# Splitting the fp32-to-bf16 weight casts into smaller DMAs and issuing them at other places of an eight-core attention and FFN layer

## What is computed

```python
xn = layernorm(x)                                   # x: (4, 2048, 2048)
nq  = rmsnorm(xn @ w_cq);  nkv = rmsnorm(xn @ w_ckv)
q = concat(nq @ w_dq_nope, rope(nq @ w_dq_rope))    # 16 heads, 128 + 64
k = concat(nkv @ w_dk_nope, rope(xn @ w_k_rope))
v = (nkv @ w_dv) / sqrt(16 * 128)
s = softmax(causal(q @ k.T / sqrt(192))) @ v @ w_proj
h = xn @ W1.T;  q = clip(round(h / 0.1), -32768, 32767)
g = silu(gelu(q * 0.1) @ W2.T)                      # W1: 8192 x 2048, W2: 2048 x 8192
out = x + s * g
```

## Time and profile before

| | us |
|---|---|
| median of 2 runs | 8458.27 (8431.25 to 8485.28) |
| the profiled execution | 8322.42 |
| its span, slowest core (core 1) | 8320.8 |
| spans of the 8 cores | 8282.9 to 8320.8 |
| P1, from the barrier of Pm1 to the first `dknB` load of P1end | about 105 to 1276 |
| P1end, from the first matmul | about 1300 to 2024 |
| P2 of pass 0, and of pass 1 | 2087 to 3378, 5034 to 5947 |

### The profile page before, as it was taken

One profiled execution on the slowest core, in us unless ns is written; L12 is line 12 of the kernel. 1 busy time (PEld: TensorE's weight loads), 2 busy tenths in 40 slices (PEclk: granted clock), 3 DMA queues, 4 the chain that ended last, 5 costly groups with the idle time before them and its releaser, 6 DMA issues.

```text
span 8320.8 us, 74648 instructions; the slowest of 8 cores (8282.9 to 8320.8 us)
## 1 busy us (share of the span) xinstructions
PE 5338.5 (64%) x23280; PEld 2334.2 (28%) x23280; DVE 2314.3 (28%) x4548; ACT 1242.8 (15%) x2969; POOL 472.5 (6%) x571
## 2 busy tenths in 40 slices
PE   0413034554676678866666758999977767676776
PEld 0201011222232233323222323444323332332332
DVE  1101022223233334023333214344213333333321
ACT  0101001112000001011111101111012222222220
POOL 1000000000121211000000000000000000000000
PEclk9766567787888899976666779999976666666678
DMA  6598883221554443421111242222331101110114
GB/s 124 77 112 123 120 116 83 70 74 67 145 138 136 126 132 97 132 79 53 53 53 52 80 154 69 75 76 74 105 97 37 35 21 37 37 34 23 37 46 156
DMA packets 372685, 698.02 MB, mean 84 GB/s; under 512 B 161248, under 2 KB 251360, under 8 KB 364960
## 3 DMA queue, kind: packets, MB, share of 16 engines
q1 hardware_dynamic: 335104, 504.76, 20.3%
q0 software_dynamic: 37200, 188.51, 14.5%
HBM read 740.59 MB, written 178.78 MB: 110 GB/s over the span
## 4 chain that ended last, share of the span: by engine, by line
PE 52%; DMA 18%; DVE 12%; issue 6%; ACT 5%; another core or an unknown queue 5%; POOL 1%; DVEq 0%; SPq 0%; ACTq 0%; POOLq 0%
PE pb L766 5%; PE pb L772 4%; PE pb L693 4%; PE pb L699 4%; PE pb L368 4%; PE pb L370 4%; PE pb L372 4%; PE pb L1014 3%; DVE heap L977 3%; DMA heapb<-cqB 3%; PE pb L1032 2%; PE pb L959 2%; PE pb L950 2%; ACT heap L990 2%
## 5 line engine op out<-in xcount | busy, mean ns | idle before, releaser
L368 PE MATMUL pb<-heapb 128*128 128x512 bf16 (+1 forms) x1920 | 755.8, 394 | 424.9 <-DMA heapb<-dknB 283.7
L766 PE MATMUL pb<-heapb 128*128 128x512 bf16 x2048 | 796.0, 389 | 330.8 <-DMA heapb<-w2B 240.7
L379 DVE TENSOR_TENSOR heapb<-pb,heapb 128x128 bf16<-128x128 f32 (+1 forms) x1600 | 523.6, 340 | 1170.6 <-ACT heapb L377 546.5
L693 PE MATMUL pb<-heapb 128*128 128x512 bf16 x2048 | 785.2, 383 | 52.5 <-DMA heapb<-w1B 52.5
L772 PE MATMUL pb<-heapb 128*128 128x512 bf16 x2048 | 794.8, 388 | 0.8 <-POOL heapb L744 0.8
L699 PE MATMUL pb<-heapb 128*128 128x512 bf16 x2048 | 784.7, 383 | 0.0
L377 ACT ACTIVATE heapb<-pb 128x128 bf16<-128x128 f32 (+1 forms) x1600 | 488.8, 316 | 1839.7 <-PE pb L1014 1005.3
L370 PE MATMUL pb<-heapb 128*128 128x512 bf16 (+1 forms) x1920 | 753.2, 392 | 0.0
L372 PE MATMUL pb<-heapb 128*128 128x512 bf16 (+1 forms) x1920 | 750.5, 391 | 0.0
L437 PE MATMUL pb<-heap 128*128 128x128 f32 x384 | 86.7, 419 | 957.5 <-ACT heap L429 957.5
L1014 PE MATMUL pb<-heap 128*128 128x128 f32 x1280 | 457.7, 399 | 275.6 <-DVE heap L1003 275.6
(11 more groups left out here) (141 smaller groups left out, 6238.8 us busy)
## 6 DMA issues: line engine op xcount, KB each, us to landing
heapb<-w1B SPq DMA_DIRECT2D x128, 512.0 KB, 3.6
heapb<-w2B SPq DMA_DIRECT2D x512, 128.0 KB, 2.2
heapb<-prB SPq DMA_DIRECT2D x128, 512.0 KB, 4.6
heapb<-cqB SPq DMA_DIRECT2D x128, 384.0 KB, 3.8
w1B<-w1s POOLq DMA_DIRECT2D x16, 2048.0 KB, 169.6
w2B<-w2t POOLq DMA_DIRECT2D x4, 8192.0 KB, 201.6
heapb<-kkB SPq DMA_DIRECT2D x64, 512.0 KB, 3.3
heapb<-vvB SPq DMA_DIRECT2D x64, 512.0 KB, 4.7
```

What stands on the lines that cost most here:

```text
L368: p.do("tensor", lambda e: e.matmul(bank_ap, wh_ap, xh_ap, start=first, stop=False), reads=list(wbufs) + list(xbufs), writes=[pbank[n]], a ...
L379: p.do("vector", lambda e: e.tensor_tensor(lo_ap, bank_ap, hi_ap, ALU.subtract), reads=[pbank[nb], hibuf], writes=[lobuf])
L693: p.do("tensor", lambda e, kc=kc, fg=fg, bk=bk: e.matmul(banks[bk][:, 0:512], bv("AB", A_W1 + 2048 * (fg % 3) + 128 * kc, A_W1 + 2048 * (f ...
L766: p.do("tensor", lambda e, kc=kc, tt=tt: e.matmul(banks[2 + tt][:, 0:512], bv("AB", A_AP + 512 * kc + 128 * tt, A_AP + 512 * kc + 128 * (t ...
```

## The change

The 24 casts of `cast_gx` become 50, and are issued elsewhere. Sizes below are of the bf16 result. W1 stays in 16 casts of 2 MB, W2 goes from 4 of 8 MB to 16 of 2 MB, the query weights from 6, 6 and 3 MB to ten of 1.5 MB, and the projection from one of 8 MB to 8 of 1 MB. The bytes are the same.

- 12 casts of W1: one behind each token tile 4 to 15 of P1.
- The other 4 of W1: at the end of heads 0 to 3 of P1end. The 16 of W2: one at the end of heads 4 to 11, two at the end of heads 12 to 15.
- The query and projection casts: at the end of the slabs of P2 in pass 0, two each after slabs 0 to 4, three each after slabs 5 and 6, two after slab 7.

The semaphores are counted over new sets (GXA to GXF), and SyncE waits for the second half of W1 in slab 3, ahead of the load for slab 4's first block, and for the second half of W2 in slab 4. SyncE, PE, ACT and DVE keep their instructions and their order.

```diff
+            if t >= 4 and gx_p1:
+                sx, dx, semx = gx_p1.pop(0)
+                cast_gx(sx, dx, semx)
...
-        if grp == 0:
-            for fg in range(0, 64, 4):
-                cast_gx(w1t_d[fg:fg + 4], w1B[fg:fg + 4], "GXA")
-            gx_marks["w1"] = ("GXA", p.cnt.get("GXA", 0))
-        elif grp == 1:
-            for r in range(0, D_FF, 2048):
-                cast_gx(w2t_d[r:r + 2048, :], w2B[r:r + 2048, :], "GXB")
...
-        elif grp == 2:
-            cast_gx(w_cq_d[:, :], cqB[0], "GXC")
-            cast_gx(w_dqn_d[:, :, :], dqnB[0], "GXC")
-            cast_gx(w_dqr_d[:, :, :], dqrB[0], "GXC")
...
-        else:
-            cast_gx(w_pr_d[:, :], prB[0], "GXD")
...
         store(krotB[1, h], bs("AB", 0, 64, A_KROTP + 2048, A_KROTP + 4096), krotp)
+        if gx_p1:
+            sx, dx, semx = gx_p1.pop(0)
+            cast_gx(sx, dx, semx)
+        elif gx_p1end:
+            sx, dx, semx = gx_p1end.pop(0)
+            cast_gx(sx, dx, semx)
+            if h >= 12 and gx_p1end:
+                sx, dx, semx = gx_p1end.pop(0)
+                cast_gx(sx, dx, semx)
...
+                    if g == 0 and fg + 2 == 32:
+                        p.raw_wait("sync", "GXB", p.cnt.get("GXB", 0))
...
+                if g == 0 and slab == 4 and nt == 0:
+                    p.raw_wait("sync", "GXD", p.cnt.get("GXD", 0))
...
+            if g == 0:
+                for _ in range(2 if slab < 5 else 3):
+                    if gx_p2a:
+                        sx, dx, semx = gx_p2a.pop(0)
+                        cast_gx(sx, dx, semx)
+                    elif gx_p2b:
+                        sx, dx, semx = gx_p2b.pop(0)
+                        cast_gx(sx, dx, semx)
```

More of the change, by code:

```diff
@@ L357, in build_program @@
     cast_weight(w_dv_d[:, :, :], dvB[0])
-    gx_marks = {}
     def cast_gx(src_fp32, dst_bf16, sem):
@@ L363, in cast_gx @@
              reads=[], writes=[], dma=sem)
+    gx_p1 = []
+    for fg in range(0, 64, 4):
+        gx_p1.append((w1t_d[fg:fg + 4], w1B[fg:fg + 4], "GXA" if fg < 32 else "GXB"))
+    gx_p1end = []
+    for i2 in range(16):
+        r2 = 512 * i2
+        gx_p1end.append((w2t_d[r2:r2 + 512, :], w2B[r2:r2 + 512, :], "GXC" if i2 < 8 else "GXD"))
+    gx_p2a = []
+    for i2 in range(4):
+        gx_p2a.append((w_cq_d[32 * i2:32 * (i2 + 1), :], cqB[0, 32 * i2:32 * (i2 + 1), :], "GXE"))
+    for h2 in range(0, 16, 4):
+        gx_p2a.append((w_dqn_d[h2:h2 + 4], dqnB[0, h2:h2 + 4], "GXE"))
+    gx_p2a.append((w_dqr_d[0:8], dqrB[0, 0:8], "GXE"))
+    gx_p2a.append((w_dqr_d[8:16], dqrB[0, 8:16], "GXE"))
+    gx_p2b = []
+    for i2 in range(8):
+        gx_p2b.append((w_pr_d[16 * i2:16 * (i2 + 1), :], prB[0, 16 * i2:16 * (i2 + 1), :], "GXF"))
     if stop_here("PW"):
@@ L679, in build_program @@
                 if g == 0:
-                    p.raw_wait("sync", *gx_marks["w1"])
+                    p.raw_wait("sync", "GXA", p.cnt.get("GXA", 0))
                 w1_load(0)
@@ L757, in build_program @@
                 if g == 0 and slab == 0 and nt == 0:
-                    p.raw_wait("sync", *gx_marks["w2"])
+                    p.raw_wait("sync", "GXC", p.cnt.get("GXC", 0))
+                if g == 0 and slab == 4 and nt == 0:
+                    p.raw_wait("sync", "GXD", p.cnt.get("GXD", 0))
                 w2_load(0)
@@ L806, in build_program @@
         if g == 0:
-            p.raw_wait("sync", *gx_marks["cq"])
+            p.raw_wait("sync", "GXE", p.cnt.get("GXE", 0))
         cq_load(0)
@@ L881, in build_program @@
         if g == 0:
-            p.raw_wait("sync", *gx_marks["dq"])
+            p.raw_wait("sync", "GXE", p.cnt.get("GXE", 0))
         load_dq(0)
@@ L1065, in build_program @@
         if g == 0:
-            p.raw_wait("sync", *gx_marks["pr"])
+            p.raw_wait("sync", "GXF", p.cnt.get("GXF", 0))
         pr_load(0)
```

3 lines of the change are left out of this document (removed).

## The result

| | before | after |
|---|---|---|
| profiled execution, us | 8322.42 | 8427.14 |
| its span, slowest core, us | 8320.8 (core 1) | 8425.5 (core 7) |
| median of 25 and of 26 runs, us | 8448.35 | 8482.13 |
| ratio after to before | | 1.0096, 95% [1.0058, 1.0134] |

The kernel is 1.0% slower by the ratio. The profiled spans differ by 105 us, where the sum of the prediction was +100.

The account below looks back on a forecast made before the run. It took the start to be bound by transfers, the long rest by PE and its feeders. P1 -371, P1end and P1b +320, P2 +151 made +100: 8422 us profiled, 8560 forecast after adding 1.2%, range 8270 to 8720.

Parts of the forecast that it names:

- P1: P1: with fewer casts queued, DVE's waits for split loads and the first `dknB` load's delay go, -371 us, range 350 to 385.
- A single cast costs a head 17.6 us: P1end: one cast behind a head delays the next head's `dknB` pair by 0 to 17.6 us, upper end taken.
- The second load is caught: P1end: the second `dknB` load of a pair, issued after the first landed, lands only as the cast ends.
- the upper end for 10 of 12 heads: P1end: 10 of 12 heads with one cast pay the full 17.6 us, 176 us in all.
- the pairs of casts: P1end: two casts cost 37 us at each of heads 13, 14 and 15, 111 us in all.
- about 1010: Sign in P1end: the stage grows from 726 to about 1010 us; under 830 would favour late start or hiding.
- P1b +33: P1b: the two casts behind head 15 delay its `xq` loads, to near 41 us, +33 us.
- P2: P2 of pass 0: casts delay the next split's load, 18 us a slab for six; slabs 6, 7 add 26, 17; +151 us.
- The late start: Rival in P1end: both `dknB` loads land before the cast moves data; net -149 us, 8173 profiled; chance 0.20.
- Hiding: Rival: P1end's DMA is 0.21 busy, so 20 casts fit by volume; 8000 us profiled; chance 0.08.
- Amplification: Rival in P2: one late split drags GpSimd, DVE and SyncE, 40 us a slab; 8589 us with all heads caught; chance 0.20.
- the rule of the Trainium skill that the prediction set aside: Cast length: 2.0 us plus bytes over 436 GB/s, 6.8 us per 2 MB result; sum about -240 us; no chance given.

Follow-up runs that it names:

- experiment 2: Changed kernel with W1's and W2's casts cut into 1024-element-wide halves of twice as many rows, same bytes and places; ratio to the kernel before 0.9823, 8195 to 8237 us.
- 6: Changed kernel with P1's casts issued behind each group's last token load, four in each of groups 0 to 3; 8253 and 8293 us.
- Experiment 5: Changed kernel with one query cast behind slabs 0 to 5, two behind 6 and 7, projection casts moved to attention heads; 8391 to 8446 us.
- experiment 1: Changed kernel with P1end's casts issued only after the head's `dknB` (and `dvB`) loads have landed; ratio to the kernel before 0.9819, 8208 to 8229 us.
- 10: Changed kernel with two `dknB` buffers loaded one head ahead, high and low loads on separate semaphores; 8174 to 8239 us.

## Why the prediction was right

The forecast was +100 us on the profiled execution and the spans gave +105; 8560 us stood 0.9% above the median of 8482, inside 8270 to 8720, and "within 2%" was the likeliest case. Of the 78 us of that miss 10 come from the base, 8458 in two runs where all 25 have 8448, and about 20 from the sum, which said 1.012 where the ratio says 1.0096. The rest lies in the medians of all executions, whose quotient is only 1.0040. By its steps:

- **P1: right.** 347 us without the first `dknB` load, where 352 were predicted; the waits of 176.6, 167.0 and 8.4 us are gone and the splits' own round trips stayed. That the token loads meet casts as they did before held too: 21.52, 28.03 and 29.86 us of waits for `xnat` where there were 21.90, 31.20 and 33.33. Experiments 2 and 6 show what that is worth: another 70 to 90 us.
- **A single cast costs a head 17.6 us: right in size, wrong in which load and in how many.** Measured 18 to 19 us. "The second load is caught" fell; the first is, though it is issued 0.4 us ahead of the cast. Little decided between them. In the heads with one cast on cores 0, 4 and 7 the cast's first packet starts 2.6 to 3.8 us after the cast's issue, when 29 to 56 of the load's 128 packets have started; alone, the 128 take 1.5 us to start (from 2.0 to 3.5 us after the load's issue, kernel before). I estimate from these that with the cast about half a microsecond later the first load would have passed and the second been caught, as predicted and at the same price, and that for both to pass it would have had to come some 2 us later. The step "the upper end for 10 of 12 heads" was too small: a load that is issued beside the cast every time is caught every time, and all twelve pairs of core 7 have issues of 20.5 to 24.0 us. Twelve by 18.5 is 222 us where 176 stood. With the pairs of casts, 3 by 35 for the 111 predicted, that makes 327, and from the first matmul P1end grew from 725 to 1049 us, 324; "about 1010" was named.
- **P1b +33: right,** at +34.
- **P2: mechanism right, a little too dear.** The first parts of slabs 1 to 6 lost 13 to 18 us on core 1 where 18 were predicted, which makes 95 instead of 108; slab 6's second part +30 for 26, slab 7's +17 for 17. The sum of these is 142 of 151; as other parts came out shorter, P2 grew by 135 on core 1, and by 119 on core 7. Experiment 5 shows the late split as the cause, since half the burst costs 2 us.
- **The late start fell.** The cast moves data before either load has landed: heads of 1027 to 1054 us on six cores and 945 and 950 on two, against 830 at most by that rival. For both loads to pass, the cast's packets would have had to begin some 2 us later, by the numbers in the point on the single cast.
- **Hiding fell as `after` stands,** by the same number, but its idea of free volume was not empty. Experiments 1 and 2 hide about 70 and 57 per cent of P1end's cost of some 300 us without changing a byte. What the share of 0.21 left out is who stands beside the transfer and in what turns.
- **Amplification fell:** 24.39 us of wait in the first split of slab 2, 7.47 in the next, and 13 to 18 us a slab on core 1 (9 to 18 on core 7), not 40.

On the rule of the Trainium skill that the prediction set aside ("DMA: Bandwidth & Descriptors", Anatomy of one DMA), the trace after the change disagrees again, with medians of 16.0 to 23.5 us to landing for a 2 MB cast on the eight cores. Its other rule, that an engine takes turns between queues a packet at a time (Queues, rings and completion order), is borne out by the packets above, of which one of the load passes for each one of the cast, and by experiment 2: the same cast in packets of 2048 bytes lets a 128 KB load land after 5 to 8 us instead of 18 to 24. So the turn was the right picture for this rival, and the length of a turn, 4.6 us, was what decided it.

Open: why the casts' packets take 2.4 us on cores 4 and 5 of `after`, and on 0 and 1 in experiment 5, and up to 4.7 on the others. Both cores of a pair show it and it moves between executions of equal code, which speaks for something that cores share, perhaps whether their casts coincide. In experiment 1, where the casts stand elsewhere, they take 2.8 to 3.2 us on all eight cores. No run tried the cause.

## What to carry to other kernels

A background transfer is priced by what is issued within its length, not by its share of the DMA engines: give it a place just behind the landing of a stage's critical load (experiment 1), cut its rows small (2), and keep the loads and stores that something waits for out of the queue behind it (10 shows what they cost there). Spreading one large burst evenly over many short, latency-bound steps here only moved its cost from a few long waits (347 us of P1) to many small ones (305 us of P1end). When a load is made early, look at what shares its semaphore, since the second of a pair then starts later than its buffer allows.

## What was not expected of the hardware

- A 2 MB cast lands after 16.0 to 23.5 us with rows of 16384 elements and after 19.7 to 24.4 with rows of 1024 (medians of the eight cores), but a SyncE load of 128 KB issued beside it takes 18 to 24 us on most cores in the one case and 5 to 8 in the other.
- A load issued 0.4 us ahead of a cast is overtaken by it (23.11 us instead of 3.9), so being first in time protects nothing in another queue: 80 of its 128 packets get through at once, and the others go one for each packet of 4.6 us of the cast.
- On one pair of cores the packets of the same casts take 2.43 us where they take up to 4.6 on the others, and a load beside them 14.4 us where it takes 21.7, in one execution on one pair and in the next on another.
